# A two-lane kernel gets two more lanes: the next embedding and the next back's entry

## The reference

```
x1  = x + diag(softmax(Q K^T / sqrt(512), axis=1)) * V       # Q, K, V of layernorm(x): the "embedding"
h   = layernorm(x1)
2 x:  q,k,v = shift(h) @ wqkv; l2norm, rotary; local attention (8 heads of 64, windows of 64)
      h = h + o @ wo;  h = h + (a * gelu(g)) @ w2 + b2       # a, g from layernorm(shift(h)) @ w1
x2  = x1 + h
x3  = x2 + causal_attention(layernorm(x2))                   # 16 heads of 8
n   = layernorm(x3)
out = x3 + sum over the top 2 of 8 experts (by softmax(n @ gate_w)) and a shared one: (silu(n w_gate) * (n w_up)) @ w_down
```

## Time and profile before

| | |
|---|---|
| time, median of 3 | 1767.19 us (1765.77 to 1770.94) |
| the profiled execution | 1764.6 us, of which the span from first to last instruction is 1762.2 us |
| busy: PE, DVE, ACT, POOL | 1541.2, 1233.2, 942.4, 598.1 us (87, 70, 53, 34%) |
| x2 written (L1258), sequences 1, 0, 2 ... 7 | 225, 283, 461, 667, 876, 1079, 1284, 1559 us |
| x3 written (L1334), backs 0 to 7 | 419, 627, 836, 1040, 1241, 1433, 1605, 1698 us |

### The profile page before, as it was taken

How to read it: one execution, slowest core, us unless ns; L and a number is a source line. 1 busy time by engine, 2 the same in 40 slices (tenths; PEclk the granted TensorE clock), 3 DMA queues, 4 the chain that set the end, 5 groups by cost and what they waited for, 6 DMA issues and landing times.

```text
span 1762.2 us, 29615 instructions
## 1 busy us (share of the span) xinstructions
PE 1541.2 (87%) x11563; PEld 909.4 (52%) x11632; DVE 1233.2 (70%) x2636; ACT 942.4 (53%) x1766; POOL 598.1 (34%) x401
## 2 busy tenths in 40 slices
PE   5789876899988899888998999989998889888988
PEld 2355543545554555645555455555555446534555
DVE  6957768776588657885587865886678547875634
ACT  3566653466553864547445566448643553453451
POOL 1946727152070611625034520616106115110000
PEclk8989998899999999999999999999999999999999
DMA  4200100310150101601123101411014102404102
GB/s 127 69 1 22 28 1 21 74 29 3 44 117 21 23 17 36 134 2 24 33 69 85 24 2 43 109 36 24 25 37 105 24 1 75 106 21 91 48 2 65
DMA packets 37290, 80.11 MB, mean 45 GB/s; under 512 B 6782, under 2 KB 22654, under 8 KB 33776
## 3 DMA queue, kind: packets, MB, share of 16 engines
q1 hardware_dynamic: 37152, 78.22, 17.9%
HBM read 54.74 MB, written 8.78 MB: 36 GB/s over the span
## 4 chain that ended last, share of the span: by engine, by line
PE 52%; DVE 24%; ACT 17%; issue 4%; POOL 3%; DMA 0%; SPq 0%; POOLq 0%; DVEq 0%; ACTq 0%
PE ps L507 47%; PE ps L512 5%; ACT bigs L1025 4%; ACT work L943 4%; DVE bsmall L1316 4%; DVE fsmall L1198 2%; DVE work L1161 2%; DVE work L1160 2%; DVE fsmall L1190 1%; DVE fsmall L1168 1%; POOL fsmall L1445 1%; ACT L977 1%; ACT L979 1%; POOL work L1468 1%; DVE fsmall L1202 1%
## 5 line engine op out<-in xcount | busy, mean ns | idle before, releaser
L1445 POOL TENSOR_TENSOR fsmall<-fsmall,consts 128x8 f32<-128x8 f32 (+1 forms) x140 | 202.5, 1457 | 265.5 <-DVE fsmall L1100 254.8
L507 PE MATMUL ps<-bxt,mw 128*128 128x512 f32 x504 | 250.2, 606 | 11.4 <-ACT bigs L1051 8.4
L507 PE MATMUL ps<-maskb,identb 128*128 128x128 bf16 (+1 forms) x1119 | 222.7, 236 | 29.6 <-ACT work L943 16.9
L1468 POOL TENSOR_TENSOR work<-work 128x1024 f32<-128x1024 f32 x56 | 134.1, 2395 | 283.7 <-DVE work L1161 283.6
L943 ACT ACTIVATE work<-ps,fsmall 128x128 f32<-128x128 f32 x448 | 164.5, 512 | 48.9 <-DVE fsmall L1202 48.8
L1316 DVE TENSOR_REDUCE bsmall<-ps 128x1 f32<-128x512 f32 (+3 forms) x308 | 177.0, 631 | 10.4 <-PE ps L507 10.0
L507 PE MATMUL ps<-wqkv,h 128*128 128x512 f32 x336 | 161.7, 610 | 13.6 <-ACT vs L903 6.8
L1499 POOL TENSOR_TENSOR work<-work,fsmall 128x1024 f32<-128x1024 f32 x56 | 106.3, 1898 | 185.3 <-DVE fsmall L1193 185.3
L1025 ACT ACTIVATE bigs<-ps 128x512 f32<-128x512 f32 x280 | 148.4, 661 | 19.0 <-PE ps L507 18.3
L512 PE MATMUL ps<-ident,work 128*128 128x128 f32 x924 | 135.9, 288 | 22.2 <-ACT work L943 13.3
L507 PEld LDWEIGHTS ps<-maskb,identb 128*128 128x128 bf16 x1152 | 111.3, 99 | 59.9 <-issue 57.1
(11 more groups left out here) (335 smaller groups left out, 2967.7 us busy)
## 6 DMA issues: line engine op xcount, KB each, us to landing
mw<-in_experts SPq DMA_DIRECT2D x63, 384.0 KB, 3.1
pks<-scr_partsb SPq DMA_DIRECT2D x42, 192.0 KB
pqs<-scr_partsb SPq DMA_DIRECT2D x126, 64.0 KB
v2s<-vs SPq DMA_DIRECT2D x14, 512.0 KB, 4.4
v2s<-vs SPq DMA_DIRECT2D x14, 384.0 KB, 5.8
scr_partsb<-bigs SPq DMA_DIRECT2D x7, 768.0 KB, 5.3
wqkv<-in_experts SPq DMA_DIRECT2D x9, 384.0 KB, 3.2
xin<-in_x SPq DMA_DIRECT2D x7, 256.0 KB, 3.5
```

What stands on the lines that cost most here:

```text
L507: return nc.tensor.matmul(o, a, b, start=start, stop=stop, skip_group_check=True)
L1445: return nc.gpsimd.tensor_tensor(out, x, consts[:, k:k + 1].broadcast_to([x.shape[0], x.shape[1]]), op)
L1468: nc.gpsimd.tensor_tensor(R.qk[:, m, :], R.qk[:, m, :], R.part[m % 2], ALU.add).then_inc(R.l_add.sem, 1)
```

## The change

- A third lane, E, holds the embeddings of sequences 1 to 7, and a fourth, N, the entries of backs 1 to 6. `ORDER` is written anew for all five engines with four letters; `beside`, `ahead` and `ENTRY_AFTER` are gone.
- The embedding of the lane E (`beside=True`) can run next to the front of the sequence before it. So it has one PSUM bank, the fourth of lane F, for everything (`eb = [fb[3]] * 4`), its input and x1 alternate between two buffers, its turned x, q and k lie in `kts`, and its exponentials in `work2`. Steps that shared nothing before now wait for each other: k's matmul for q's eviction, v's for k's, each score tile for the exponential of the one before it.
- New waits against the front beside it: the first turn waits for the last turned probabilities of front s-1 (`l_pta`), V for its last value product (`l_pv`), the write of h for its last residual (`l_h2`), the load of x for x2 of s-2; `project` of layer 0 waits before v for x2 of s-1.
- The last layer's feed-forward uses three banks (`gate_bank`, `linear_bank`), and `out` uses bank 2.
- The entry waits for the second norm and the second turn of the back before.
- The chains are split (`fe`, `bn`), and GpSimd's norm steps have plain signals.
- `back_constants` waits for the entry's normalised rows before its clears.

```
-def both_lanes(front, back, fronts, front0, backs, back7):
+def all_lanes(front, back, embed, enter, fronts, front0, backs, back7):
...
-    return (chain(rounds(front, fronts), rounds(back, back7)), chain(rounds(front, front0), rounds(back, backs)))
+    return (chain(rounds(front, fronts), rounds(back, back7)), chain(rounds(front, front0), rounds(back, backs)),
+            rounds(embed, fronts), chain.from_iterable(enter(backs, s) for s in range(1, backs.count)))
...
-        self.xin, self.x1, self.fxn = rows
+        self.fxn = rows[2]
+        self.xin, self.x1 = (rows[0:2], rows[0:2]) if beside else ([rows[0]], [rows[1]])
+        self.eb = [self.fb[3]] * 4 if beside else self.fb
...
+        def gate_bank(l, c):
+
+            return (2 * c % 4, (0, 2, 1)[c])[l == LAYERS - 1]
+
+        def linear_bank(l, c):
+
+            return ((2 * c + 1) % 4, (1, 0, 2)[c])[l == LAYERS - 1]
...
             def embed(R, s):
                 yield "tp"
+                if R.beside and s:
+                    pe.wait_ge(R.l_pta.sem, R.l_pta.at(s - 1, 4 * LAYERS))
...
+                if R.beside:
+                    yield "kv"
+                    pe.wait_ge(R.a_qk.sem, R.a_qk.at(s, 1))
+                mm(R.eb[2], aw[:, 1, :], R.axt).then_inc(R.a_qkv.sem, 1)
                 yield "av"
+                if R.beside:
+                    pe.wait_ge(R.a_qk.sem, R.a_qk.at(s, 2))
...
+                    elif R.beside:
+                        pe.wait_ge(R.a_e.sem, R.a_e.at(s, b))
...
                 yield f"v01.{l}"
+                if l == 0 and s:
+                    pe.wait_ge(R.f_x2.sem, R.f_x2.at(s - 1, 1))
...
+                if R.beside and s:
+                    act.wait_ge(R.l_h2.sem, R.l_h2.at(s - 1, LAYERS))
...
+                if R.beside and s:
+                    dve.wait_ge(R.l_pv.sem, R.l_pv.at(s - 1, 8 * LAYERS))
...
             def back_constants(R):
+                pool.wait_ge(R.b_xn.sem, R.b_xn.at(0, 1))
                 for r in range(2):
                     i = nc.gpsimd.memset(R.pq_words[r], 0.0)
...
-                if not is_first(s):
-                    sp.wait_ge(R.a_x1.sem, R.a_x1.at(s - 1, 1))
+                if s > 1:
+                    sp.wait_ge(R.f_x2.sem, R.f_x2.at(s - 2, 1))
+                if s:
                     load_x(R, s)
```

More of the change, by code:

```diff
@@ L61 @@
[L61 to L65, removed]
@@ L88 @@
+        "FBFBFBFFFFFBFFFFFFFFFFFFFFF"
     ),
     "vector": (
[L90 to L93, removed]
@@ L112 @@
+        "FFFBFFFBFBFF"
     ),
@@ L138, with run_lanes @@
 EXP_AT = exp_places()
-ENTRY_AFTER = {"ln": 0, "xn": 1, "tp": 2, "q": 3, "k": 4, "v": 5, "parts": 5, "parts1": 5, "parts2": 6, "parts3": 6, "va": 5,
-               "save": 7}
 ENTRY_BANKS = [2, 2, 2, 2]
[L148 to L171, removed]
+def run_lanes(engine, order, front_lane, back_lane, embed_lane, entry_lane):
+    lanes = {"F": front_lane, "B": back_lane, "E": embed_lane, "N": entry_lane}
     for lane in lanes.values():
@@ L681, in attend @@
                 for c in range(HC):
-                    i = mm(R.fb[2], w2[:, l, c, :], R.hg[:, c, :], start=(c == 0), stop=(c == HC - 1))
+                    i = mm(R.fb[0 if l == LAYERS - 1 else 2], w2[:, l, c, :], R.hg[:, c, :], start=(c == 0), stop=(c == HC - 1))
                 i.then_inc(R.l_w2.sem, 1)
             def front(R, s):
-                yield from embed(R, s)
+                if not R.beside:
+                    yield from embed(R, s)
                 yield from project(R, s, 0)
@@ L822, in back @@
                 i.then_inc(R.r_l.sem, 1)
-                yield from beside(experts(R, s), enter(R, s + 1) if follows(R, s) else iter(()))
+                yield from experts(R, s)
             def experts(R, s):
@@ L858, in experts @@
                 down(ALL - 1)
-            run_lanes(pe, ORDER["tensor"], *both_lanes(front, back, fronts, front0, backs, back7))
+            run_lanes(pe, ORDER["tensor"], *all_lanes(front, back, embed, enter, fronts, front0, backs, back7))
         @block.scalar
@@ L998, in front @@
                 if R is front0:
-                    yield from ahead(enter(backs, 0))
+                    yield from enter(backs, 0)
             def enter(R, s):
@@ L1051, in experts @@
                         nc.scalar.activation(R.silu[k % 3], R.bb[n % banks][:, :], ACT.Silu).then_inc(R.m_silu.sem, 1)
-            run_lanes(act, ORDER["scalar"], *both_lanes(front, back, fronts, front0, backs, back7))
+            run_lanes(act, ORDER["scalar"], *all_lanes(front, back, embed, enter, fronts, front0, backs, back7))
         @block.vector
@@ L1423, in experts @@
                 add_expert(ALL - 1)
-            run_lanes(dve, ORDER["vector"], *both_lanes(front, back, fronts, front0, backs, back7))
+            run_lanes(dve, ORDER["vector"], *all_lanes(front, back, embed, enter, fronts, front0, backs, back7))
         @block.gpsimd
@@ L1514, in front @@
                 if R is front0:
-                    yield from ahead(enter(backs, 0))
+                    yield from enter(backs, 0)
             def enter(R, s):
-                R.bp.start()
                 yield "ln"
-                rstd(s, 1, R.b_stats, R.bmv, R.brs, R.bp, R.b_rstd)
+                rstd(s, 1, R.b_stats, R.bmv, R.brs, R.b_var, R.b_rstd)
                 if is_first(s):
@@ L1527, in back @@
                 yield "ln2"
-                rstd(s, 2, R.b_stats, R.bmv, R.brs, R.bp, R.b_rstd)
-                finish(R.bp)
-                if follows(R, s):
-                    yield from ahead(enter(R, s + 1))
-            run_lanes(pool, ORDER["gpsimd"], *both_lanes(front, back, fronts, front0, backs, back7))
+                rstd(s, 2, R.b_stats, R.bmv, R.brs, R.b_var, R.b_rstd)
+            run_lanes(pool, ORDER["gpsimd"], *all_lanes(front, back, embed, enter, fronts, front0, backs, back7))
         @block.sync
```

248 lines of the change are left out of this document (138 added, 110 removed).

## The result

The changed kernel takes 1709.9 us (median of 4, 1706.5 to 1714.8) against 1766.5 us on the same chip; the ratio is 0.9674, 95% interval 0.9655 to 0.9692. A second set on another chip gave 1707.0 us and 0.9658 (0.9638 to 0.9678). Forecast were 1739 us, a change of -28; it is -57.

A forecast was written before the change was run, and what follows sets the result against it. PE was taken as the bound, 1541 us of work with 221 us idle. The terms -20 - 8 - 3.5 - 2 + 5 = -28.5 us gave 1736, or 1739 us as median; 8-in-10 range 1702 to 1782.

The forecast's parts named there:

- The start: Up to the first maxima of back 0: less PE idle time, -8 us without the clears, -3.5 with them.
- The clears: GpSimd's clears wait for the entry's `normalise`, which they slowed: -3.5 us at the start, -2 at back 7.
- The periods: Five repeating periods: 4 us less each in maxima and scores, -20 in all, against +5 for function switches.
- DVE's relief in the maxima: Backs 1 to 4: 13 rotary or square-sum steps moved behind `maxturn.1`, taking 17.6 us of DVE work from the maxima.
- the signs that I had named: Right if first `normalise` takes 1.1 to 1.4 us, PE's wait there falls to about 5, and tables load 129 times.
- The one on back 1's maxima: Sign of being right: back 1's maxima take less than 50 us, with DVE busy below 42 us of them.
- x3 of two backs in a row: Sign on the period: 196 to 204 us apart if right, 206 or above if wrong.
- The end: Last stretches: only the clears at back 7's entry were counted, -2 us.
- The switches: ScalarE's function switches beside the experts: 20 more, 25.7 us of ScalarE, of which a fifth, +5 us, would count.
- rival (4): Large gain: PE reaches 87% at the start and 93% in the periods; 1690 to 1722 us, chance 0.17.
- Rival (1): The forecast itself: PE's idle time shrinks by 10 to 15%, 1722 to 1757 us, chance 0.45.
- The slower rival: Rival (3): the embedding's single-bank waits hold PE and switches cost, outweighing the gains; worked out as 1790 us, chance 0.18.

The follow-up runs named there:

- the kernel with the old end: The changed kernel with the old order of lanes F and B from the last expert of back 4 on: 1732.6 us, ratio to before 0.9799.
- The kernel with the old last stretch: The changed kernel with the old order only from the last expert of back 5 on: 1718.1 us, ratio to before 0.9698.
- the old middle: The changed kernel with the old order of lanes F and B, embedding hoisted, in backs 0 to 4, between new start and new end: 1771.5 us.
- the hoist alone, fronts start early: Changed code, old order of lanes F and B, embedding hoisted, first projections of fronts 2 to 7 laid 3 to 14 us earlier against lane B: 1817.6 us.
- the hoist alone: The changed kernel's code with lanes F and B ordered against each other as before, embedding hoisted: 1805.9 us, ratio to before 1.0214.
- both shifts undone: The changed kernel with front ends (`w2`, `out`) laid earlier and next fronts' starts later against lane B, as in the old order: 1738.8 us.

## Why the prediction was off

*The start* was right: -11.5 forecast, 11.6 us shorter and 11.9 us less idle time measured. *The clears* were right in size (3.5 us at the start in the changed kernel, 6 us in all in the kernel before) and low at back 7, 3.9 us for 2. By the Trainium skill (GPSIMD Engine Reference, Key points), GpSimd contends with VectorE's instructions in a 2-port mode or with two SBUF inputs, so a clear should run free beside a clear: the trace agrees, VectorE's take 1.76 us alone (the kernel before) and beside GpSimd's (the changed one).

*The periods* came near the sum, 20.4 us shorter for -20 + 5, by a step that failed. I wrote that DVE's relief in the maxima would let maxima and scores run at 91% of PE instead of 86.6%, and used the experts' 93% only as a far bound. DVE got no relief: its work in the maxima of backs 1 to 4 fell by 9.1 us, not 17.6, and as the stage shrank with PE's moved work, its share rose from 86 to 89%, with PE at 88% before and after. Of the signs that I had named, the 129 loads came, and `normalise` and PE's wait at the first entry fell, the wait further than forecast. The one on back 1's maxima (under 50 us, DVE under 42) came only in windows that begin with DVE's first maximum (46 and 39.8); from PE's first step it is 50.4 and 43.8. And x3 of two backs in a row came 193.7 to 206.8 us apart, two of five within my 196 to 204 and one above the 206 that was to speak against me. The signs that did come show that work was moved, not that time was won by it. The kernel with the new order in maxima and scores alone wins nothing, and the one with it in the experts alone wins nearly all. What won is in the experts: the embedding had been the filler between expert steps, the hoist takes it away (39 us slower), and the new order puts the front's end and the next front's start there, evenly. I passed over the experts because they had the least idle share, and yet that stretch is twice as long as the others and its Silu waits, 8.4 us, fell the most. That the loss and the gain lie there is shown by the runs; that they come from the missing filler, and not from other parts of the new code, is argued from the orders and the waits.

*The end* is the term that was mis-sized: I had only the clears there, -2. It is 22.2 us shorter in the trace, 11.4 us of idle and 10.8 of busy time, and the kernel with the old end is 23 us slower than the changed one. Front 7 beside back 5, and back 7 beside back 6, were laid anew as well, and I had read the order strings only for backs 1 to 4. In the kernel before, back 6's experts ended 16 us ahead of back 7's; in the changed one both end within 2 us. (The kernel with the old last stretch has the 16 us again and loses 8.)

*The switches* were priced about right (+5 for 20; 23 cost 1 to 7). *PE's busy time* fell by 8.2 us, for which I had no term; it is in the end, and its cause is open.

*The range.* The time lies where rival (4) had it, 1690 to 1722, but not by its means: PE was busy for 92% of the periods, near its 93%, and for 78% of the start to the first maxima, not 87%, and the end was not in it. Rival (1) contradicts itself: 10 to 15% of 221 us are 22 to 33 us, while 1722 to 1757 stands for 10 to 45. It was 46 us, 21%.

*The slower rival* was real: the hoist without the new order takes 1805.9 us. Its mechanism was mostly not the one I gave: the embedding's exponentials on one bank cost PE 4.3 us with the old middle and 0.5 in the changed kernel's periods, while PE's idle time among the experts went from 37 to 55 us with the hoist, in the place that the embedding had left.

## What to carry to other kernels

When a latency-bound chain is moved out of a stretch, ask what it was filling: it may be the cover of another chain there, and the move pays only if something else is put in its place. Read the new order in every stage where it differs, above all in those that occur once (the end), and place a gain by switching the order stage by stage; shorter stages show where work went, not where time was won. Begin and end a stage at the same steps of the same engine before and after, or a shift between two engines looks like a gain. A sum that comes out right does not prove its steps.

## What the runs showed of the hardware

The same matmuls, in another order alone, kept PE busy for 1532.9 us at a mean granted clock of 0.977 (the changed kernel) and for 1578.1 us at 0.956 (the hoist alone, fronts start early). Idle time by itself doesn't tell the clock: it was 0.961 with 243 us of PE's idle time (the hoist alone), 0.970 with 221 (before), 0.968 with 195 (old end) and 0.977 with 175 (changed), but also 0.977 with 208 (both shifts undone). In the stretch from 283 to 331 us, ahead of the first maxima, PE was busy for 28.5 of 48 us at a mean clock of 0.68 before, and for 30.3 of 44 us at 0.77 after. Within these stretches the clock stood at its lower level (0.50, 1.2 of 2.4 GHz) from 290 to 297 and from 311 to 325 us before, the first time behind 7 us without any work of PE, and after the change only from 299 to 313 us. Within one kernel the time follows the clock: the changed kernel's second set ran at 1704.3, 1704.0, 1709.7 and 1712.6 us with 0.981, 0.980, 0.976 and 0.974. What sets the clock of an order was not tested.
